# A layer on one core: weighted values of a whole row in 32x64 tiles into four banks, values spread by way of DRAM, x loaded a pass ahead, new orders of issue

## What is computed

```python
# x: (32, 128, 128), cond: (32, 64), mask: (32, 128)
y   = moe(x, cond)                       # 8 experts of 64, the 2 best per token, and a shared one of 128
a   = banded_attention(y)                # 128 features, span 32, no softmax, layer norm, weight and bias
x1  = x + a
xn  = _ln(x1) * g_norm
q   = l2norm(heads(xn @ Wq)) * q_scale   # 16 heads of 64
k,v = split(xn @ Wkv)                    # one key and value head, shared by the 16
k,v = prepend(null_kv, k, v)             # 129 keys
p   = softmax(8 * q @ l2norm(k).T + bias, causal, mask)
z   = _ln(concat_heads(p @ v) @ Wout) * g_out
h   = silu(z @ w1) * (z @ w2)            # 512 hidden
out = x1 + gelu(gelu(h @ h1) @ h2) @ w3
```

## Time and profile before

| | |
|---|---|
| runs | 832.1 us median of 3 (830.48 to 832.76) |
| the profiled execution | 828.2 us, span 826.5 us |
| mean granted TensorE clock | 0.946 |
| PE busy | 720.0 us, 87% |
| DVE, ACT, POOL busy | 575.9, 520.1 and 356.9 us (70, 63 and 43%) |
| longest waits of PE | 57.0 us in 7 for `xl` (L1050); 12.8 us in 1 for the routing's first product |
| DMA | 27.31 MB, 11.3% of the engines' time on the queue of SP |

### The profile page before, as it was taken

One profiled execution on the slowest core, in us unless ns is written; L12 is line 12 of the kernel. 1 busy time (PEld: TensorE's weight loads), 2 busy tenths in 40 slices (PEclk: granted clock), 3 DMA queues, 4 the chain that ended last, 5 costly groups with the idle time before them and its releaser, 6 DMA issues. The chain is left out here.

```text
span 826.5 us, 18078 instructions
## 1 busy us (share of the span) xinstructions
PE 720.0 (87%) x6080; PEld 576.1 (70%) x6080; DVE 575.9 (70%) x1735; ACT 520.1 (63%) x1519; POOL 356.9 (43%) x395
## 2 busy tenths in 40 slices
PE   3969388849997999979997999979996999999997
PEld 3846256637885677857885687757884768877897
DVE  3586299649784878759783978669783899595532
ACT  2224177417982688637982679537872578789954
POOL 3013664633454534363544534364545343854200
PEclk9799699969999899989999999989998899999999
DMA  7012310130004000210004000310003000000000
GB/s 253 1 31 76 103 52 2 25 83 2 0 2 116 5 2 1 72 48 2 0 4 116 2 2 1 75 46 2 1 16 104 2 1 2 20 22 1 14 2 13
DMA packets 47786, 27.31 MB, mean 33 GB/s; under 512 B 22592, under 2 KB 45264, under 8 KB 47312
## 3 DMA queue, kind: packets, MB, share of 16 engines
q1 hardware_dynamic: 47392, 26.15, 11.3%
q10 hardware_dynamic: 304, 0.01, 0.0%
HBM read 19.71 MB, written 2.24 MB: 27 GB/s over the span
## 5 line engine op out<-in xcount | busy, mean ns | idle before, releaser
L701 POOL TENSOR_TENSOR sb_sm<-sb_sm,sb_rden 128x128 f32<-128x128 f32 (+3 forms) x128 | 97.1, 764 | 230.5 <-DVE sb_rden L1177 230.4
L800 ACT ACTIVATE sb_sm<-sb_sm,sb_nmx 128x65 f32<-128x65 f32 (+3 forms) x512 | 178.2, 352 | 16.5 <-DVE sb_nmx L1173 16.1
L1166 DVE SCALAR_TENSOR_TENSOR sb_sm<-ps_S,sb_rq,sb_biasm 128x65 f32<-128x65 f32 (+3 forms) x512 | 112.2, 292 | 9.6 <-PE ps_S L1416 8.0
L683 POOL TENSOR_TENSOR sb_rq<-sb_qss,sb_mhalf 128x16 f32<-128x16 f32 x32 | 93.6, 2947 | 53.9 <-DVE sb_qss L1150 53.9
L693 POOL TENSOR_TENSOR sb_biasm<-sb_bias,sb_maskn 128x128 f32<-128x128 f32 (+3 forms) x128 | 109.1, 871 | 15.9 <-DVE sb_sm L1166 11.8
L800 ACT ACTIVATION_READ_ACCUMULATOR sb_sm<-sb_sm,sb_nmx 128x1 f32 x512 | 96.6, 189 | 0.0
L1294 PE MATMUL ps_M<-sb_xh,sb_wguh 128*128 128x512 f32 x78 | 39.0, 500 | 58.8 <-DVE sb_xl L1050 57.0
L1440 PE MATMUL ps_S<-sb_pT,sb_vblk 64*128 64x128 f32 (+1 forms) x896 | 83.3, 329 | 6.5 <-DVE sb_pT L1189 6.1
L1440 PEld LDWEIGHTS ps_S<-sb_pT,sb_vblk 64*128 64x128 f32 x896 | 70.1, 188 | 25.3 <-issue 11.1
L1453 PEld LDWEIGHTS ps_z<-sb_wout,sb_oT 128*128 128x128 f32 x512 | 62.9, 192 | 9.5 <-issue 6.0
L1453 PE MATMUL ps_z<-sb_wout,sb_oT 128*128 128x128 f32 x512 | 67.4, 279 | 0.0
(11 more groups left out here) (260 smaller groups left out, 1810.1 us busy)
## 6 DMA issues: line engine op xcount, KB each, us to landing
sb_hA<-routes SPq DMA_DIRECT2D x48, 128.0 KB, 3.6
sb_vblk<-sb_vs SPq DMA_DIRECT2D x128, 32.0 KB, 1.9
sb_xg<-in_xT SPq DMA_DIRECT2D x8, 256.0 KB, 3.3
sb_xs<-in_x SPq DMA_DIRECT2D x8, 256.0 KB, 3.6
sb_qs<-in_xT SPq DMA_DIRECT2D x1, 2048.0 KB, 10.8
sb_hA<-in_h SPq DMA_DIRECT2D x2, 1024.0 KB, 5.0
out_y<-sb_res SPq DMA_DIRECT2D x7, 256.0 KB, 3.7
sb_rows<-in_rows SPq DMA_DIRECT2D x1, 648.0 KB, 5.5
```

The lines of the kernel that those rows point to most:

```text
L683: pool.tensor_tensor(rq[:, cut], qss[:, cut], mhalf[:], ALU.pow).then_inc(q_rnorm.sem, 1)
L701: pool.tensor_tensor(p, p, stat(rden, g, j).unsqueeze(2).broadcast_to([128, 4, wide - 1]), ALU.mult)\
L800: ins = act.activation(p[:, t], p[:, t], ACT.Exp, bias=least[:, t:t + 1], accum_out=total[:, t:t + 1])
L1166: ins = dve.scalar_tensor_tensor(scored(g, j)[:, t], bank(g, "sim", n, odd)[:, first:first + wide], rq[:, col:col + 1], masked_bias(j % 4) ...
```

## The change

Weighted values. `pv` is one step a row, not two. It waits for the four transposes of the row and takes all four S banks. The 32 matmuls are in tiles of 32 rows by 64 columns: 32-key block c of the weights (partitions 32c to 32c+31) goes to bank c, heads of even and odd number to the lower and upper 64 partitions; per query block i the moving side is (4-i) x 64 columns. `p_turn` writes `pT` in another order, now with two slots of a whole row, and for block 3 in two transposes, where it was one. `ot_copy` has two activations of 128x256 per step, where it had one of 128x512. The weights of the output projection are laid out for it on the host, and `z_proj` takes its four blocks in another order.

Values. `vblk` with its zeros and its memset goes. `store_values` (`vst`) writes `vs` to DRAM in two transfers, `spread_values` (`vb`, now for each half of the group) reads them back in one each, the same values on four strips of 32 partitions. The first half is free after the second row's weighted values of the group before, the other after its last.

Loads. `load_x`, the rows (`load_rows`, `ls`) and the mask (`lm`) are steps of stage W, two groups ahead of the pass, where they were one ahead.

Orders. All orders are new, but PE's and DVE's in the drain.

```diff
@@ ORDER (fill and steady passes; start, seventh, last likewise)
     "pe fill": """
-        lg.0 warm.0-5 lg.1-6 pb.0 rw.0 lg.7 pb.1 exp.0-4 down.0 pb.2 warm.6 qkv.0 scores.0 pb.3 warm.7 mix.0
-        warm.8-11 fl.0 warm.12-13 fl.1-2 warm.14 wr.0 warm.15 xnT.0 warm.16-17 q.0-1 kv.0 q.2-4 qs.0-3 q.5-7
-        kT.0 qs.4-7 warm.18-21
+        lg.0 warm.0-6 lg.1 pb.0 lg.2-3 pb.1 lg.4-7 rw.0 exp.0 pb.2 exp.1-2 pb.3 exp.3-4 down.0 qkv.0 scores.0
+        warm.7 mix.0 warm.8 fl.0 warm.9-13 fl.1 wr.0 fl.2 warm.14-16 xnT.0 warm.17 kv.0 q.0-4 qs.0-3 q.5-7 kT.0
+        warm.18 qs.4-7 warm.19-21
     """,
     "pe steady": """
-        sim.0-1 exp.0-4 down.0 sim.2 zT.0 sim.3 qkv.0 l1.0 sim.4 l1.1 PV.0 l1.2-3 scores.0 PV.1 sim.5 l2.0-3
-        mix.0 z.0 l3.0-2 sim.6-7 xnT.0 l3.3 z.1 kv.0 q.0-1 PV.2-4 q.2-3 l4.0 q.4 z.2 PV.5 qs.0-3 PV.6-7 z.3
-        q.5-7 z.4 kT.0 qs.4-7 z.5-7
+        sim.0 exp.0-3 sim.1 exp.4 down.0 zT.0 sim.2-3 qkv.0 l1.0 sim.4 l1.1 sim.5 l1.2-3 scores.0 l2.0-3 mix.0
+        PV.0 l3.0-2 sim.6-7 xnT.0 l3.3 z.0 q.0 z.1 kv.0 PV.1 q.1-2 l4.0 PV.2 z.2 q.3-4 qs.0-3 q.5-7 z.3 kT.0
+        qs.4-7 z.4 PV.3 z.5-7
     """,
     "sp fill": """
-        vb.0 maskn.0 rw.0 hw.0 wr.0
+        ls.0 wr.0 hw.0 lx.0 lm.0 vst.0 vb.0-1
     """,
     "sp start": """
-        maskn.0 rw.0 hw.1 vb.0 wb.0
+        lx.0 hw.1 vst.0 wb.0 lm.0 vb.0-1 ls.0
     """,
     "sp steady": """
-        rw.0 maskn.0 wb.0 l4.0 vb.0
+        lx.0 vst.0 vb.0 lm.0 wb.0 l4.0 vb.1 ls.0
     """,
     "sp seventh": """
-        maskn.0 rw.0 vb.0
+        vst.0 vb.0-1
     """,
...
-STAGE |= {"wb": "W"}
+STAGE |= {"wb": "W", "lx": "W", "ls": "W", "lm": "W"}
...
     if step == "PV":
-        return "SS" if k % 2 == 0 else ""
+        return "SSSS"
...
-        vblk = sb("vblk", [128, GB, 4, 2 * DH])
+        vrep = sb("vrep", [128, 2, 4, 2 * DH])
...
-        pT, oT = sb("pT", [128, RING, TURNED]), sb("oT", [128, NP, S])
+        pT, oT = sb("pT", [128, 2, TURNED]), sb("oT", [128, NP, S])
...
-        DRAINED |= {("PV", n // 2 * 2, n % 2): (ot_copied, n + 1) for n in range(2 * GB)}
+        DRAINED |= {("PV", n // 4, n % 4): (ot_copied, n // 2 + 1) for n in range(4 * GB)}
...
             def load_x(g, k):
-                if g == 0:
-                    return
                 sp.wait_ge(x_low.sem, x_low.at(g, 0))
                 sp.dma_start(xg[:], a["xT"][:, g * GT:(g + 1) * GT]).then_inc(x_loaded.sem, 16)
+
+            def load_rows(g, k):
                 sp.wait_ge(own_x.sem, own_x.at(g, 0))
...
-            def spread_values(g, k):
+            def store_values(g, k):
                 sp.wait_ge(v_shifted.sem, v_shifted.at(g, 1))
-                if g == 0:
-                    sp.wait_ge(v_cleared, 1)
-                sp.wait_ge(pv_psum.sem, pv_psum.at(g, 0))
-                for i in range(4):
-                    for c in range(4):
-                        sp.dma_start(vblk[c * QW:(c + 1) * QW, :, i, c % 2 * DH:(c % 2 + 1) * DH], vs[i * QW:(i + 1) * QW])\
-                            .then_inc(v_spread.sem, 16)
+                for spread in v_spread:
+                    sp.wait_ge(spread.sem, spread.at(g, 0))
+                for half in range(2):
+                    sp.dma_start(values[half].rearrange("q i d -> i q d"), vs[:, 2 * half:2 * half + 2].rearrange("p b d -> p (b d)"))                        .then_inc(v_stored.sem, 16)
+
+            def spread_values(g, half):
+                sp.wait_ge(v_stored.sem, v_stored.at(g, 32))
+                sp.wait_ge(pv_psum.sem, pv_psum.at(g, 2 * half - 2))
+                src = bass.AP(tensor=values.tensor, offset=half * S * 2 * DH, ap=[[0, 4], [8 * DH, QW], [1, 8 * DH]])
+                sp.dma_start(vrep[:, half].rearrange("p i d -> p (i d)"), src).then_inc(v_spread[half].sem, 16)
...
-            pool.memset(vblk[:], 0.0).then_inc(v_cleared, 1)
...
             def ot_copy(g, n):
-                half = oT[:, n % 2 * 4:n % 2 * 4 + 4].rearrange("p t (i q) -> p i t q", i=4)
-                act.wait_ge(pv_psum.sem, pv_psum.at(g, n // 2 * 2 + 2))
+                act.wait_ge(pv_psum.sem, pv_psum.at(g, n // 2 + 1))
                 act.wait_ge(z_psum.sem, z_psum.at(g, n - 1))
-                act.activation(half, bank(g, "PV", n // 2 * 2, n % 2)[:].rearrange("p (i t q) -> p i t q", i=4, t=4),
-                               ACT.Identity, bias=nval).then_inc(ot_copied.sem, 1)
+                for c in (n % 2 * 2, n % 2 * 2 + 1):
+                    ins = act.activation(oT[:, c::4].rearrange("p m (i q) -> p i m q", i=4),
+                                         bank(g, "PV", n // 2, c)[:, 0:256].rearrange("p (i m q) -> p i m q", i=4, m=2),
+                                         ACT.Identity, bias=nval)
+                ins.then_inc(ot_copied.sem, 1)
...
             def pv(g, k):
+                ps = [free(g, "PV", k, c, (v_spread[k // 2], 16), (p_turned, 4 * k + 4)) for c in range(4)]
+                buffer = pT[:, (g * GB + k) % 2].rearrange("p (u m n q) -> p u m n q", m=2, n=2, q=QW)
+                for i in range(4):
+                    units = slice(UNITS[i], UNITS[i] + 4 - i)
+                    for c in range(4):
+                        rows = slice(c * QW, (c + 1) * QW)
+                        for odd in range(2):
+                            ins = pe.matmul(ps[c][odd * DH:(odd + 1) * DH, i * 2 * QW:256], vrep[rows, k // 2, i, k % 2 * DH:k % 2 * DH + DH],
+                                            buffer[rows, units, :, odd], start=(i == 0), stop=(i == 3), skip_group_check=True)
                 ins.then_inc(pv_psum.sem, 1)
...
             def z_proj(g, n):
-                for c in range(n % 2 * 4, n % 2 * 4 + 4):
+                for c in [m * 4 + n % 2 * 2 + i for m in range(2) for i in range(2)]:
```

More of the change, by code:

```diff
@@ L118 @@
[L118 to L121, removed]
+        rw.0 xl.0 pl.4 exp.0 sim.0 exp.1 max.0 exp.2 max.1 exp.3 inv.0 sim.1 exp.4 max.2 sim.2 max.3 inv.1
@@ L122 @@
+        max.4-5 inv.2 down.0 tp.0-1 inv.3 sim.3 tp.2 max.6 qkv.0 scores.0 inv.4 tp.3-4 max.7 mix.0 sim.4 inv.5-6
+        max.8 ln1.0 inv.7 tp.5 max.9 sim.5 ln2.0 tp.6 max.10 inv.8 tp.7 max.11 xnT.0 inv.9 sim.6 tp.8 max.12
+        inv.10 tp.9 inv.11 max.13 kv.0 sim.7 inv.12-13 max.14 tp.10 max.15 tp.11 q.0 tp.12 inv.14 maskn.0 tp.13
+        inv.15 tp.14 kT.0 tp.15 vs.0 q.1-3 pl.5 q.4-5 ssq.0 ssc.0 q.6-7
     """,
     "dve steady": """
-        xl.0 ln3.0 sim.0 exp.0 max.0 exp.1-3 max.1 sim.1 exp.4 max.2 zT.0 inv.0-1 down.0 max.3 zl.0 sim.2 inv.2
@@ L125 @@
[L125 to L128, removed]
+        xl.0 ln3.0 sim.0 exp.0-2 max.0 exp.3 max.1 sim.1 exp.4 max.2 zT.0 inv.0 max.3 tp.0 inv.1 down.0 zl.0
@@ L129 @@
+        sim.2 max.4 tp.1 max.5 qkv.0 sim.3 inv.2 l1.0-1 inv.3 h1.0-1 inv.4 l1.2 tp.2 l1.3 h1.2 max.6 h1.3 max.7
+        tp.3 scores.0 inv.5 tp.4 sim.4 max.8 tp.5 inv.6 sim.5 tp.6 inv.7 max.9 h2.0 tp.7 h2.1 mix.0 h2.2-3
+        max.10-11 ln1.0 inv.8 maskn.0 ln2.0 tp.8 sim.6 inv.9 xnT.0 inv.10 tp.9 sim.7 max.12 tp.10 max.13 q.0
+        kv.0 inv.11-12 tp.11 max.14-15 kT.0 q.1-2 l4.0 tp.12 vs.0 inv.13 q.3 inv.14 q.4 tp.13 q.5 tp.14 inv.15
+        q.6 tp.15 ssq.0 ssc.0 q.7
     """,
     "dve seventh": """
-        xl.0 ln3.0 sim.0 exp.0-3 max.0 sim.1 max.1-3 exp.4 sim.2 zT.0 down.0 inv.0-1 zl.0 tp.0 max.4 inv.2 max.5
@@ L136 @@
+        zT.0 inv.3 tp.0-1 down.0 max.5 zl.0 sim.3 tp.2 max.6 inv.4 qkv.0 max.7 tp.3-4 inv.5 sim.4 tp.5 l1.0-1
+        sim.5 h1.0 max.8 scores.0 inv.6-7 h1.1 max.9 l1.2 tp.6 l1.3 max.10 mix.0 h1.2 tp.7 h1.3 ln1.0 sim.6
+        ln2.0 inv.8 h2.0 maskn.0 inv.9 xnT.0 tp.8 max.11-13 q.0 h2.1 inv.10 tp.9 q.1-2 sim.7 q.3 kv.0 max.14
+        q.4-5 h2.2 max.15 tp.10 h2.3 q.6 kT.0 inv.11 ssq.0 inv.12-13 tp.11 inv.14-15 q.7 tp.12-13 ssc.0 tp.14
+        vs.0 tp.15
     """,
     "dve last": """
-        sim.0 max.0 sim.1 ln3.0 inv.0 max.1-2 zT.0 max.3 tp.0 sim.2 inv.1 max.4 zl.0 max.5 tp.1 inv.2 l4p.0
@@ L390, in layer_kernel @@
         routes = nc.dram_tensor("routes", (B * E, S), fp32, kind="Internal").ap()
+        values = nc.dram_tensor("values", (2, QW, 4, 2 * DH), fp32, kind="Internal").ap()
         toeplitz = nc.dram_tensor("toeplitz", (HEADS, 2 * S), fp32, kind="Internal").ap()
@@ L1179, in p_turn @@
             def p_turn(g, j):
-                n, (i, wide, _) = j // 2, unit(j % 4)
+                k, (i, wide, _) = j // 4, unit(j % 4)
                 if (g, j) == (0, 0):
```

133 lines of the change are left out of this document (57 added, 76 removed).

## The result

The changed kernel takes 732.33 us (median of 4 runs, 731.88 to 735.29) against 832.43 for the kernel before in the same comparison: ratio 0.881, 95% interval 0.878 to 0.884. The forecast was 749 with 722 to 778, so the time lies inside the range, 17 us under the forecast. The profiled execution took 735.3 us (span 733.6), the slowest of the four and 3.0 above the median.

A forecast was written before the change was run, and what follows sets the result against it. PE bounds each pass, and a late SP queue every boundary. The terms -57 - 6 - 25 + 7 + 2 + 3 - 7 = -83 take 828.2 to 745.2 us, plus 3.9 for the median: 749, range 722 to 778.

The forecast's parts named there:

- x a pass ahead: Pass boundaries: loading x two groups ahead removes PE's 57.0 us wait, and 13 us of low clock behind it.
- DVE back: Pass boundaries: about 1 us each comes back as PE waiting on DVE, +7 us for seven.
- A row of weighted values: PE's `pv`: 32 small-tile matmuls take 1.50 us a row instead of 2.39, -25 us over 28 rows.
- Four banks: `pv` taking all four S banks: PE waits 0.25 us a row for ACT's copies, +7.0 us for 28 rows.
- DVE's transposes: One 128x512 transpose becomes two of 128x256: +0.7 us of DVE a pass, half showing where DVE sets the pace, +2 us.
- rival 2: `pv`: the four banks cost their full 1.0 us a row, giving 770 us; chance 0.18.
- Routes late: SP's queue: the routes' load behind the values' first store and load costs 0.5 us on six passes, +3 us.
- Fill: Fill: `xnT` starts 3.6 us earlier, and moving the position bias gives about 3.4 more, -7 us, between 0 and -12.
- 1: `pv`: two tiles of one row strip take turns, a row stays at 2.2 to 2.4 us, giving 774 us; chance 0.17.
- 4: SP's queue: the load of x is still late, behind `vb.1`, giving 806 us; chance 0.02.
- 5: `pv`: 32x64 tiles run one at a time or nearly, slower than before, 986 us if one by one; chance 0.02.
- Rival 3: `pv` and fill: tiles overlap better, 1.25 us a row, and the fill gives 12 us, giving 737 us; chance 0.11.

The follow-up runs named there:

- e9: Kernel before, with x, its rows and mask loaded two groups ahead and the first pass's h1, h2 and routes loads ahead of the 16 value copies: 761.78 us.
- e10: Changed kernel with the values spread by 16 direct copies, issued behind the routes' load, in place of the way by DRAM: 729.33 us.
- e7: Changed kernel with the fill's orders of PE, ACT, DVE and POOL as in the kernel before, SP's kept new: 734.30 us.
- e5: Changed kernel with half the moving columns in each of the 32 matmuls of the weighted values: 733.73 us in a single run.
- e3: Changed kernel with every matmul of the weighted values issued twice a row: 777.42 us.
- e6: Changed kernel with the routes' load ahead of the store of the values on SP in the steady passes: 730.54 us.
- e4: Changed kernel with the two inner loops of the weighted values swapped, so successive matmuls go to different row strips: 732.27 us.

## Why the prediction came out as it did

The sum was made for a profiled execution: -83, where the spans give -92.9 (826.5 to 733.6). So 9.9 of the 17 us are the sum's. The other 6.9 are the step from the profiled execution to the median: I added 3.9, as the kernel before has it, and it is -3.0 here. The spread of single executions doesn't carry over from one kernel to the next.

By passes, a steady one was forecast at 82.5 us, with 80 to 84 as the sign, and takes 79.6. The spans of e9 and e10 split the 92.9: SP's order alone 67.4 (826.5 to 759.1), tiles and the other engines' orders 31.6 (to 727.5), and the changed kernel's way of the values with the routes behind it gives 6.1 back (to 733.6; 3.0 in the medians). Of the 6.1 only 2.5 lie in the five passes; 2.2 lie in the fill, whose length differs by as much among kernels with the same orders (e7 above). The forecast had -63 for the first, -23 for the second (the rows' -25, the banks' +7, the transposes' +2 and the fill's -7), +3 for the third.

**x a pass ahead** (-57 - 13 + 7 = -63; measured -67.4): right in its mechanism, while part of the agreement is luck. The seven waits, 57.0 us in all, went whole. The slow matmuls and all else gave 10.4 where 13 were counted, and the 7 of DVE did not come. In the kernel before, 12.46 of them end the fill and 14.91 the first pass, which is why these two fell by 12.7 and 15.5 in e9, and the steady ones by 7.2, their wait of 5.6 to 5.9 and the slow matmuls behind it. What the prediction passed over is that `hw` and `wb` stood behind the same 16 copies: without moving them 20 us of the gain don't come (781 for 762). The diff moved them, so the sum did not suffer; the reasoning did. The step "late next" looked at POOL and DVE, and not at the other items of the same queue.

**DVE back** (+1 a boundary): not there. With the old orders PE waited for DVE 2.3 us a pass (e9), 1.5 of it at the turn of x, but that wait stood in the kernel before too; at the boundary there was none. In the changed kernel both are 0 in the steady passes.

**A row of weighted values**: forecast 1.50 for 2.39, measured 1.35 on the same scale, in all but one of the 28 rows behind the first pass. The 28 rows of the sum thus save 29 us and not 25. The price "44 to 52 ns a matmul, whatever their columns" came near with its 1.41, by luck: the same 32 matmuls take 0.95 us with half of the columns (e5), 30 ns each. Columns count: 640 a tile more cost 1.21 us (e3), near the 1.11 of the column price, and 320 fewer save 0.40 (e5). In the steady pass PE's busy time fell from 83.03 (e9) to 79.59 us (e10), 3.4; with the idle 2.3 that is the 5.7 by which the passes differ, 28.3 over five of them. Summed from the start of each record to the next, the weighted values take 10.02 us of e9's pass and 5.41 of e10's, 4.6 less, and PE's other steps 1.2 more.

**Four banks** (+7) and **DVE's transposes** (+2): 0 in the steady passes. Together they are 9 us that never showed. ACT's copies took longer than I took them (0.47 us for 0.40), 60.8 us of ACT's work a pass as against 61.9, and still PE waited for them once, 1.1 us in the first pass. The orders keep other PE work behind every row; rival 2 had priced a wait without looking where in the new order it would stand.

```profile
L817 ACT ACTIVATE sb_oT<-ps_S,sb_cols 128x256 f32<-128x256 f32 x128 | 52.5, 470 | 28.3 <-PE ps_S L1439 20.2
```

**Routes late** (+3): right in place, in waits of DVE of 0.6 to 1.0 us in three passes, and about right in size: the five passes of e6 are together 2.6 us shorter. The medians say 1.8 (e6) and 3.0 (e10), and their intervals overlap with the changed kernel's. The landing (5.3 for 3.6) used up more of the margin than the estimate had.

**Fill** (-7): wrong. The turn of x stood at 68.48 and was forecast near 61.5; it came at 66.18, and no earlier because DVE finished its input at 66.13, where that had been there at 64.84 before:

```profile
62.87 3.26 DVE L1084 TENSOR_SCALAR sb_hT<-sb_x,sb_mv,sb_rstd 128x128 f32<-128x128 f32 x4 [0.73 <-POOL sb_rstd L670]
```

So the 3.4 us from the moved position bias did not come, and 2.3 of the other 3.6 did. PE lost these again before the first expert step, which starts at 84.4 us with either order. From the turn to there the granted clock is 0.73 with the new orders and 1.00 with the old ones (e7):

```profile
66.18:84.37 18.19, 17.43 (x85) 13.35 (x85) 13.81 (x27) 8.64 (x13) 2.07 (x3) 0.73 0.28 89
...
69.17:84.43 15.26, 14.16 (x90) 10.27 (x88) 11.64 (x22) 9.59 (x14) 6.02 (x6) 1.00 0.34 110
```

The 12.9 us by which this step starts earlier than before are the first of the seven waits on x (12.46).

**First pass**: the new tiles and orders are worse there than the old ones, 67.4 us against 64.35 (e9), with the clock at 0.85 against 0.97 and PE waiting 10.0 us against 8.6; the prediction had no term for it. The fill's orders are not the reason: e7 has the old ones and a first pass of 67.1 us. A kernel with the old orders of the first pass was not run. Nor was the new tiling run with the old orders, so how the 5.7 us a pass divide between tiles and orders rests on the records of PE and not on a run.

**The rivals**: 1 fell with e4 and the records of the row, 2 with the list of waits (1.1 us on ACT's copies), 4 with the boundary, 5 with the row of 1.35 us. Rival 3, 737, is nearest by its number, but its row of 1.25 us and its 12 us in the fill are not what happened.

So the second group came out 8.6 us above its 23. It was too low by 9 for banks and transposes that never showed, by the idle 2.3 us a pass that PE no longer has (11.5 in five), which no term of the sum names, and by 4 for rows cheaper than 1.50. Against these stand the fill's 7, the first pass's 3 and the 1.2 us a pass that PE's other steps take more. The terms close only roughly: in the drain, where the sum has 7 us for eight rows, e10 is 3.9 us shorter than e9. Which of the new orders took the idle time away stays open.

The fastest kernel here that forms all sums is e10, 729.33 us: 16 plain copies, behind the routes' load. It is 3.0 us under the changed kernel, with intervals of the ratio that just overlap.

## What to carry to other kernels

When a wait on a queue is taken away, list every other item of that queue with the time at which its reader would want it now; the next ones may be late too, hidden behind the first: here 57.0 us of waits hid two of 7.1 and 9.2. The place of a transfer in its queue can matter far more than its cost: the same 16 copies cost 0 or 83 us. And an experiment whose total doesn't move is only read once its trace is: e5 saved 0.40 us a row and lost all of it to a load that came at its old time.

## What I had not expected of the hardware

Eight fp32 tiles of 32x64 run at once, near the column price of one: a row with 5120 columns takes 1.35 us, where one by one they would take 8.9. With 128 columns or more a record costs its columns, the next eight records starting 0.22, 0.16 and 0.11 us later for 256, 192 and 128; with 64 columns records start some 12 ns apart, whatever the columns would allow. With half of the columns (e5) the records of 64 and of 32 columns are both 12 ns apart, and a row comes to 15 ns a record (0.95 / 64), under the 22 that I had read from the score step as a floor.

A load's landing differs with what is queued around it: the same load of x landed in 7.2 us (median) in the changed kernel, 5.7 with the routes first (e6) and 4.1 with the 16 copies behind the routes (e10), the routes' load in 5.3, 3.7 and 3.7. Which neighbour does it was not taken apart.
